# Eight LSTM experts on one core: state halves exchanged by label, one half fed per expert, recurrent products in f32, swapped copies by DMA

## What is computed

```python
def step(carry, xt):                      # in _expert; xt is zero where expert e was not choice k
    h, c = carry
    gates = xt @ Wi + h @ Wh + b
    i_, f_, g_, o_ = jnp.split(gates, 4, axis=-1)
    c = jax.nn.sigmoid(f_) * c + jax.nn.sigmoid(i_) * jnp.tanh(g_)
    h = jax.nn.sigmoid(o_) * jnp.tanh(c)
    return ((h, c), h @ Wo + bo)
...
mask = (top_idx.T[:, None, :] == jnp.arange(E)[None, :, None]).astype(x.dtype)
expert_x = (mask[..., None] * flat_x[None, None]).reshape(K, E, S_, B_, I_)
out = run_ke(expert_x, Wi, Wh, b, Wo, bo).reshape(K, E, N, -1)
y = jnp.einsum('ken,nk,keno->no', mask, rw, out)
```

## Time and profile before

| | us |
|---|---|
| median of 3 runs | 1760.58 (1759.59 to 1762.61) |
| the profiled execution, its own time | 1761.26 |
| its span in the trace | 1759.5 |
| PE busy | 1692.6 (96%) |
| DVE busy | 1543.5 (88%) |
| ACT busy | 1000.6 (57%) |
| DMA queue of SyncE, share of 16 engines | 27.8% |

### The profile page before, as it was taken

The page is one execution under the profiler, slowest core; times in us unless marked ns, Lnnn a source line. Parts: engine busy times, 40 slices in busy tenths (PEclk is TensorE's granted clock), DMA queues, the critical chain, the costliest instruction groups (busy, mean ns, idle before and its releaser), DMA issues.

```text
span 1759.5 us, 25844 instructions
## 1 busy us (share of the span) xinstructions
PE 1692.6 (96%) x9864; PEld 822.0 (47%) x9864; DVE 1543.5 (88%) x2419; ACT 1000.6 (57%) x1124; POOL 48.8 (3%) x42
## 2 busy tenths in 40 slices
...
DMA packets 204092, 110.96 MB, mean 63 GB/s; under 512 B 125796, under 2 KB 185111, under 8 KB 203968
## 3 DMA queue, kind: packets, MB, share of 16 engines
q1 hardware_dynamic: 203888, 109.28, 27.8%
...
## 4 chain that ended last, share of the span: by engine, by line
PE 52%; DVE 33%; issue 9%; ACT 3%; DMA 1%; SPq 1%; POOL 0%; DVEq 0%; ACTq 0%; POOLq 0%
PE gates L551 40%; DVE tmp L1072 4%; PE yp L557 3%; DVE Hs L1056 3%; DVE xm L1044 3%; DVE C L1076 3%; DVE tmp L1087 2%; DVE tmp L1051 2%; DVE tmp L1066 2%; PE FA L490 2%; PE FA L475 1%; DVE z L1091 1%; ACT tmp L713 1%; DVE xn L857 1%; PE FB L463 1%
## 5 line engine op out<-in xcount | busy, mean ns | idle before, releaser
L713 ACT ACTIVATE tmp<-gates,bias_sb 128x1024 f32<-128x1024 f32 x504 | 558.6, 1109 | 444.0 <-PE gates L551 442.9
L551 PE MATMUL gates<-xm,wi_sb 128*128 128x512 f16 x3024 | 738.0, 380 | 5.3 <-ACT tmp L713 5.3
L551 PE MATMUL gates<-Hs,wh_sb 128*128 128x512 f16 x2880 | 699.9, 379 | 0.0
L551 PEld LDWEIGHTS gates<-xm,wi_sb 128*128 128x128 f16 x3024 | 291.7, 98 | 391.5 <-issue 90.8
L551 PEld LDWEIGHTS gates<-Hs,wh_sb 128*128 128x128 f16 x2880 | 281.8, 98 | 339.8
L720 ACT ACTIVATE tmp<-C 128x1024 f32<-128x1024 f32 x128 | 135.3, 1057 | 176.3 <-DVE C L1076 171.1
L1051 DVE SCALAR_TENSOR_TENSOR tmp<-tmp 128x1024 f32<-128x1024 f32 x128 | 156.5, 1222 | 42.8 <-ACT tmp L720 41.0
L1066 DVE SCALAR_TENSOR_TENSOR tmp<-tmp 128x1024 f32<-128x1024 f32 x120 | 145.4, 1212 | 51.5 <-ACT tmp L713 51.5
L1056 DVE SCALAR_TENSOR_TENSOR Hs<-tmp,Hs 128x1024 f16<-128x1024 f32 x120 | 147.0, 1225 | 15.2 <-ACT Hs L724 15.2
L1044 DVE TENSOR_TENSOR xm<-xs,masks 128x2048 f16<-128x2048 f16 x128 | 156.1, 1219 | 2.8 <-DMA masks<-mask_scratch 2.8
L1076 DVE SCALAR_TENSOR_TENSOR C<-tmp 128x1024 f32<-128x1024 f32 x120 | 147.0, 1225 | 4.1
...
## 6 DMA issues: line engine op xcount, KB each, us to landing
masks<-mask_scratch SPq DMA_DIRECT2D x128, 256.0 KB, 5.3
roww<-mw_scratch SPq DMA_DIRECT2D x128, 256.0 KB, 3.6
rowk<-mask_scratch SPq DMA_DIRECT2D x128, 128.0 KB, 2.9
...
out_dram<-h SPq DMA_DIRECT2D x16, 256.0 KB, 2.3
C<-in_wi SPq DMA_DIRECT2D x1, 2048.0 KB, 11.3
C<-in_wh SPq DMA_DIRECT2D x1, 2048.0 KB, 8.9
```

Source lines behind the costliest of these rows:

```text
L551: last = mm(gates[:, slot, k * SEQ:(k + 1) * SEQ], w, v, start=(i < K), stop=(i >= len(seq) - K))
L713: A(tmp[:, gate_at(gate, e), :], gates[:, (n - 1) % 2, :], ACT.Tanh, bias=bias_sb[:, e, gate:gate + 1], scale=UNSCALE).then_inc(s_tanh, 1)
```

## The change

The tokens' two states of an expert are no longer tied to k = 0 and k = 1. Each token has a label per expert (`lab`, 0 or 1) that says which k its first half now stands for. Where an expert is chosen through the other k, the two halves of H and C are exchanged for that token before the step, and the label flips. After that the first half is always the one that takes input and gives output.

- Input products run on 512 columns instead of 1024: three f16 matmuls per gate. The second half gets none.
- The recurrent products are f32 matmuls on the unsplit state H and unsplit weights, two of 512 columns per gate. `split_hi`, `hidden_lo` and the f16 state Hs are gone.
- The exchange: SyncE copies the state inside SBUF with halves crossed (`copy_c` into Cx, `copy_h` into Hx, two DMAs of 256 KB each per copy), and VectorE takes it with a predicated copy of 1024 columns (`swap_c`, `swap_h`) where the swap mask is set. There is one Cx and one Hx, so a copy waits for the swap of the expert before it.
- `chosen` loses its predicated copy and `rows_in` its rowk load. The mask tile holds "chosen" and "swap" in place of k = 0 and k = 1. `weights` at tick 23 makes these masks and the label with three small operations more.
- The O gate's tmp tile is single now, and its tanh waits for the hidden of the expert before. In step 0 the second half gets one matmul with a zero operand. The weights Wh are scaled in place in f32; the three instructions that made their low part (L817) are gone.

```diff
-        wh_sb = sb("wh_sb", [P, E, 2, 4 * P], f16)
+        wh_sb = sb("wh_sb", [P, E, 4 * P])
         wo_sb = sb("wo_sb", [P, E, P])
         bias_sb = sb("bias_sb", [P, E, 4])
         C = sb("C", [P, E, K * SEQ])
-        Hs = sb("Hs", [P, E, 2, K * SEQ], f16)
-        tmp = sb("tmp", [P, 7, K * SEQ])
-        masks = sb("masks", [P, 2, K, SEQ], f16)
-        xm = sb("xm", [P, 2, K, 2, SEQ], f16)
+        H = sb("H", [P, E, K * SEQ])
+        Cx = sb("Cx", [P, K * SEQ])
+        Hx = sb("Hx", [P, K * SEQ])
+        tmp = sb("tmp", [P, 6, K * SEQ])
+        masks = sb("masks", [P, 2, 2, SEQ], f16)
+        xm = sb("xm", [P, 2, 2, SEQ], f16)
...
-            return {I: e % 2, G: 2 + e % 2, F: 4, O: 5 + e % 2}[gate]
+            return {I: e % 2, G: 2 + e % 2, F: 4, O: 5}[gate]
...
+                swapped = (s - 1) * E + e - 1
+                if swapped > 0:
+                    sp.wait_ge(s_h_swap, swapped)
+                    sp.wait_ge(s_c_swap, swapped)
...
+            def copy_c(s, e):
+
+                n = (s - 1) * E + e
+                sp.wait_ge(s_c, n + 1)
+                if n:
+                    sp.wait_ge(s_c_swap, n)
+                for k in range(K):
+                    sp.dma_start(Cx[:, k * SEQ:(k + 1) * SEQ], C[:, e, (1 - k) * SEQ:(2 - k) * SEQ]).then_inc(s_c_copy, 16)
+
+            def copy_h(s, e):
+
+                n = (s - 1) * E + e
+                sp.wait_ge(s_h, n + 1)
+                if n:
+                    sp.wait_ge(s_h_swap, n)
+                for k in range(K):
+                    sp.dma_start(Hx[:, k * SEQ:(k + 1) * SEQ], H[:, e, (1 - k) * SEQ:(2 - k) * SEQ]).then_inc(s_h_copy, 16)
...
+                    if g == 0 and e < E - 1 and not first:
+                        copy_c(s, e + 1)
+                    elif g == 0 and e == E - 1 and not last:
+                        copy_c(s + 1, 0)
                     if g == 1 and e < E - 2:
                         mask_in(s, e + 2)
+                    if g == 2 and e < E - 2 and not first:
+                        copy_h(s, e + 2)
+                    elif g == 2 and e >= E - 2 and not last:
+                        copy_h(s + 1, e + 2 - E)
...
-                        pe.wait_ge(s_hlo, s * E + e - E + 1)
-                parts = [(wi_sb, lambda k, v: xm[:, e % 2, k, v, :])]
-                if not first:
-                    parts.append((wh_sb, lambda k, v: Hs[:, e, v, k * SEQ:(k + 1) * SEQ]))
-                seq = []
-                for w, mov in parts:
-                    for wpart, vpart in ((HI, HI), (HI, LO), (LO, HI)):
-                        for k in range(K):
-                            seq.append((w[:, e, wpart, gate * P:(gate + 1) * P], mov(k, vpart), k))
-                for i, (w, v, k) in enumerate(seq):
-                    last = mm(gates[:, slot, k * SEQ:(k + 1) * SEQ], w, v, start=(i < K), stop=(i >= len(seq) - K))
+                        pe.wait_ge(s_h_swap, s * E + e - E + 1)
+                rows_of = slice(gate * P, (gate + 1) * P)
+                fed, other = gates[:, slot, 0:SEQ], gates[:, slot, SEQ:2 * SEQ]
+                for wpart, vpart in ((HI, HI), (HI, LO), (LO, HI)):
+                    mm(fed, wi_sb[:, e, wpart, rows_of], xm[:, e % 2, vpart, :], start=(wpart == HI and vpart == HI),
+                       stop=(first and wpart == LO))
+                if first:
+                    last = mm(other, wi_sb[:, e, HI, rows_of], zero_in, start=True, stop=True)
+                else:
+                    mm(fed, wh_sb[:, e, rows_of], H[:, e, 0:SEQ], start=False, stop=True)
+                    last = mm(other, wh_sb[:, e, rows_of], H[:, e, SEQ:2 * SEQ], start=True, stop=True)
...
-                elif gate == O and m >= 2:
-                    act.wait_ge(s_z, m - 1)
+                elif gate == O and m >= 1:
+                    act.wait_ge(s_h, m)
...
-            def split_hi(s, e):
-                act.wait_ge(s_h, s * E + e + 1)
-                A(Hs[:, e, HI, :], tmp[:, gate_at(O, e), :], ACT.Copy, scale=V_SCALE).then_inc(s_hhi, 1)
...
+            def scale_wh():
+                act.wait_ge(s_wh_load, 16)
+                for c0, c1, half in ((0, 2, 0.5), (2, 3, 1.0), (3, 4, 0.5)):
+                    A(wh_sb[:, :, c0 * P:c1 * P], wh_sb[:, :, c0 * P:c1 * P], ACT.Copy,
+                      scale=W_SCALE * V_SCALE * 0.5 * half).then_inc(s_wh, 1)
...
-                    V.tensor_copy(mk[:, :, 0:E], K1)
-                    V.tensor_copy(mk[:, :, E:2 * E], K2)
+                    TT(mk_sel, K1, K2, ALU.add).then_inc(S["sel"], 1)
+                    if not is_zero(b):
+                        wait("sw_", b)
+                    TT(EQ, lab[:, :, :], K2, ALU.not_equal).then_inc(S["ne"], 1)
                     wait("wb", b1)
-                    TT(mw[:, :, :], IX, IX2, ALU.add).then_inc(S["mwc"], 1)
+                    TT(mw[:, :, :], IX, IX2, ALU.add)
+                    wait("sel", b1)
+                    wait("ne", b1)
+                    TT(mk_swap, EQ, mk_sel, ALU.mult).then_inc(S["mwc"], 1)
+                    wait("mwc", b1)
+                    TT(lab[:, :, :], lab[:, :, :], mk_swap, ALU.not_equal).then_inc(S["sw_"], 1)
...
+                mv_ = masks[:, e % 2, 0:1, :].to_broadcast([P, 2, SEQ])
+                TT(xm[:, e % 2, :, :], xs[:, par, :, :], mv_, ALU.mult).then_inc(s_xm, 1)
...
+            def swap_h(s, e):
+
+                n = (s - 1) * E + e
+                dve.wait_ge(s_h_copy, 32 * (n + 1))
+                V.copy_predicated(halves(H[:, e, :]), masks[:, e % 2, 1:2, :].to_broadcast([P, K, SEQ]).bitcast(u16),
+                                  halves(Hx[:, :])).then_inc(s_h_swap, 1)
+
+            def swap_c(s, e):
+
+                n = (s - 1) * E + e
+                dve.wait_ge(s_c_copy, 32 * (n + 1))
+                V.copy_predicated(halves(C[:, e, :]), masks[:, e % 2, 1:2, :].to_broadcast([P, K, SEQ]).bitcast(u16),
+                                  halves(Cx[:, :])).then_inc(s_c_swap, 1)
...
+                STT(out=H[:, e, :], in0=tmp[:, gate_at(O, e), :], scalar=1.0, in1=tmp[:, TANH_C, :],
                     op0=ALU.add, op1=ALU.mult).then_inc(s_h, 1)
...
-            def hidden_lo(s, e):
-                dve.wait_ge(s_hhi, s * E + e + 1)
-                STT(out=Hs[:, e, LO, :], in0=tmp[:, gate_at(O, e), :], scalar=V_SCALE, in1=Hs[:, e, HI, :],
-                    op0=ALU.mult, op1=ALU.subtract).then_inc(s_hlo, 1)
...
-                V.copy_predicated(at[:, 0:SEQ], rowk1[:, e % 2, :].bitcast(u16), at[:, SEQ:2 * SEQ]).then_inc(s_sel, 1)
+                dve.wait_ge(s_row_in[e % 2], 16 * (s * (E // 2) + e // 2 + 1))
+                dve.wait_ge(s_h, n + 1)
                 if n:
                     dve.wait_ge(s_y, n)
-                dve.wait_ge(s_sel, n + 1)
-                TT(z32[:, :], at[:, 0:SEQ], roww[:, e % 2, :], ALU.mult).then_inc(s_z, 1)
+                TT(z32[:, :], H[:, e, 0:SEQ], roww[:, e % 2, :], ALU.mult).then_inc(s_z, 1)
...
+                    if g == 1 and e < E - 1 and not first:
+                        swap_h(s, e + 1)
                     if t == XM_AT and not last:
                         masked_input(s + 1, 0, 1 - par, False)
+                        swap_h(s + 1, 0)
+                    if g == 3 and e < E - 1 and not first:
+                        swap_c(s, e + 1)
+                    elif g == 3 and e == E - 1 and not last:
+                        swap_c(s + 1, 0)
```

More of the change, by code:

```diff
@@ L215, in lm_tower_kernel @@
         s_whi = sem("s_whi")
+        s_wh = sem("s_wh")
+        s_hzero = sem("s_hzero")
+        s_c_copy = sem("s_c_copy")
+        s_h_copy = sem("s_h_copy")
+        s_c_swap = sem("s_c_swap")
+        s_h_swap = sem("s_h_swap")
         s_wlo = sem("s_wlo")
@@ L320, in _ @@
             load(enc_dram[P:NBJ, :], encB, s_enc_out)
-            load(wh_st.rearrange("p a (b n) -> p (a b) n", b=2), wh.rearrange("e i n -> i e n"), s_wh_load)
+            load(wh_sb[:, :, :], wh.rearrange("e i n -> i e n"), s_wh_load)
             load(wo_sb[:, :, :], wo.rearrange("e i n -> i e n"), s_wo_load)
```

78 lines of the change are left out of this document (26 added, 52 removed).

## The result

The changed kernel takes 1680.5 us (median of 4 runs, 1679.2 to 1682.0) against 1760.1 (1759.0 to 1762.6) for the kernel before: a ratio of 0.955, with its interval 0.953 to 0.956. The forecast was 1675 in a range of 1640 to 1730. The profiled execution took 1681.96 us and has a span of 1680.2, 79.3 less than before.

What follows compares the result with a forecast made beforehand. TensorE paced 15 of 16 steps, VectorE step 0; afterwards their loop binds. Savings of 62 us (fourteen steps), 12 (step 0), 4 (before it) and 8 (last step) sum to 86: 1761.3 becomes 1675, range 1640 to 1730.

Steps and rivals of the forecast that it cites:

- the loop as drawn: Steady step: four legs across TensorE, ScalarE and VectorE in a row, 105.9 us falling to 101.5; 1655 to 1695 us, chance 0.50.
- TensorE's gain: Gate units on TensorE: each falls from 2.59 to 2.36 us, 7.2 us less TensorE work per step, 105.2 to 98.0.
- The predicated copy: VectorE's swaps of H and C: 1.19 us per 1024-column copy, two per expert-step; mean duration near 1.26 us.
- Rival 4: VectorE: predicated copy with broadcast mask at half rate, 2.26 us, total 1840 us; chance 0.12 shared with Rival 3 and other losses.
- leg B: Steady step, from qkv to VectorE taking up q and k, which ScalarE makes: 5.8 us falling to 5.5.
- Leg A, TensorE from x2T: Steady step, TensorE from x2T to qkv with 11 gate units in it: 33.6 us falling to 31.1.
- first part of C: Leg C is VectorE from q and k to moments2, 60.8 us falling to 58.0; its first part precedes expert 1's gate.
- Copies: DMA copies into Cx and Hx: hidden, landing in 3.5 to 5 us, no swap waiting; 2.6 us spare at the tightest.
- Rival 3: DMA copies come late, slower from 11.2 us landing, 1845 us at 12; chance 0.12 shared with Rival 4 and other losses.
- Start and step 0: Before step 0, 4 us saved by not splitting Wh; in step 0, 12 us saved from lighter VectorE work.
- Rival 1: VectorE: copies at the upper price, 0.19 us more each, or longer legs: 1708 us; with longer waits, chance 0.21.
- Rival 2: Steady step: looser loop, TensorE alone sets it at 98.0 + 0.7 us, total 1636 us; chance 0.14.

## Why the prediction was right, and where not

**The time.** 1680.5 for 1675, the sum 79.3 for 86. The likeliest case, the loop as drawn, is the one that came. In part the terms missed to both sides: the start gave 3.3 us less than forecast, step 0 4.3 more, the steady steps 6 less. The nearness of the total owes something to that.

**TensorE's gain**: right. A unit runs from 864.52 to 866.89 in the trace after, 2.37 us for 2.36, its f32 matmuls at 0.86.

```profile
864.52 0.81 PE L578 MATMUL gates<-xm,wi_sb 128*128 128x512 f16 x3
865.17 1.02 PE L583 MATMUL gates<-H,wh_sb 128*128 128x512 f32 x2
866.03 1.02 PE L584 MATMUL gates<-H,wh_sb 128*128 128x512 f32 x2
866.89 0.81 PE L578 MATMUL gates<-xm,wi_sb 128*128 128x512 f16 x3
```

**The predicated copy**: right where it counts. From start to start it is 1.19 to 1.21 us, as below; I took 1.19 (its rows, 1.22 less 0.69, make 1.18). The mean duration of one is 1.30 to 1.32, not 1.26.

```profile
805.25 1.30 DVE L1087 COPY_PREDICATED H<-masks,Hx 128x1024 f32<-128x1024 uint16 x1
806.44 1.08 DVE L957 TENSOR_REDUCE wred<-pr 128x28 f32<-128x896 f32 x1
...
812.87 1.31 DVE L1094 COPY_PREDICATED C<-masks,Cx 128x1024 f32<-128x1024 uint16 x1
814.08 0.60 DVE L952 TENSOR_REDUCE red<-FB 128x64 f32<-128x448 f32 x1
```

The 1.13 us that the Trainium skill's "VectorE: DVE Perf Modes" gives by its section on the TRN2 errata is 0.06 to 0.08 short. Rival 4, half rate, is out.

**The loop**: the step's sum was 0.5 short (101.5 for 101.96). Read by legs it all stands in leg B, and the sentence of the working that failed there reads: "ScalarE makes them behind a gate's tanh and the cell's tanh; the latter is ready a little sooner." It was not sooner. The cell's tanh starts 2.24 us behind qkv (872.05), where before it was 1.96 (1021.80), and k comes 0.28 later with it. What went with `hidden_lo` was also cover. In the kernel before VectorE waited 0.86 us for ScalarE's split and spent 1.14 on the low part while GpSimd worked on rstd; now it waits 1.12 us for rstd, and only 0.9 of those 2.0 us are saved. The row of before, the tanh before and after:

```profile
909.14 1.23 DVE L1056 SCALAR_TENSOR_TENSOR Hs<-tmp,Hs 128x1024 f16<-128x1024 f32 x1 [0.86 <-ACT Hs L724]
...
1023.76 1.06 ACT L720 ACTIVATE tmp<-C 128x1024 f32<-128x1024 f32 x1 [0.65 <-DVE C L1076]
```

```profile
874.29 1.06 ACT L754 ACTIVATE tmp<-C 128x1024 f32<-128x1024 f32 x1 [0.93 <-DVE C L1122]
...
893.88 0.81 PE L578 MATMUL gates<-xm,wi_sb 128*128 128x512 f16 x3
```

But a longer leg B did not lengthen the step: the earlier masked input brings it to 5.06, below the forecast, and the step stays at 102.0. The 0.5 us lie in two terms of the path that binds. TensorE's way from qkv to expert 1's gate was put at 21.7 and the tanh at 1.2, 22.9 together. It is 895.23 - 872.05 = 23.18: 21.83 to the end of the gate's unit (893.88), with 2.5 for the window products put at 2.4, and 1.35 from there to VectorE's start. From that gate to moments2 the forecast left 58.0 - (22.9 - 5.5) = 40.6 for VectorE, and it is 40.82. That is 0.3 and 0.2 in each of 13.5 steps, the 6 us by which the row of the steady steps missed.

**"Leg A, TensorE from x2T"**: its length was right, its meaning was too simple. It was drawn as a loop of four legs in a row, each binding. In the changed kernel the binding loop is TensorE from x2T straight on to the gate of expert 1 (19.23 + 35.03), VectorE from there (40.82 + 6.88), 101.96 in all. Leg B and the first part of C lie beside it, 0.6 us shorter, the wait of 0.63 for that gate. So leg B as a leg was no lever. The lighter units of experts 0 to 3 show the other side: take TensorE's part of it away, and VectorE's own way round holds the step at 101.3 (101.96 less 0.63). With the units of experts 5 to 7 lighter it is VectorE's way to `rows` that holds it, at nearly the same length.

**Copies**: hidden, as forecast. They land in 2.4 to 2.6 us, not in 3.5 to 5; the figure of the row for reads from memory was taken for a copy inside SBUF. Rival 3 needed 11.2 us. "No swap waits" was wrong for one in 240. The room worked out for a copy of C, 7.6 us, comes to 7.5 from its rows (8.91 less 1.12, 0.59 and 0.83, and 1.14 more).

**Start and step 0**: 4 and 12 were forecast, 0.7 and 16.3 came. The 4.5 us of splitting Wh did go, but `rows` of step 0 is ready at 78.37 now and TensorE, on its warm-up products (L629), takes it up only at 80.75:

```profile
78.28 2.54 PE L629 MATMUL yp<-identb 128*128 128x512 bf16 x11
80.75 1.16 PE L496 MATMUL FB<-table,rows 41*128 41x128 f32 x8
```

In step 0 nearly all of the 16 us taken from VectorE arrived; from one take-up of k to the next it is 71.0 us long for 87.2 before, where 12 less would be 75 (the 78 was counted from a window of 90 us). The end gave 10.31 us per expert for 10.3.

**Rival 1** (longer waits, dearer copies) came true by a sixth of its 33 us, in the two terms of the binding path and not through the wait for rstd. **Rival 2** asked for VectorE to be no bound; taking 8.5 us off VectorE gets there.
